# Expert gates: ScalarE's positive part plus VectorE's hundredth read from PSUM, in place of a copy and a maximum within SBUF

## What is computed

```python
def _leaky(x):
    return jnp.where(x >= 0, x, LEAKY_SLOPE * x)        # LEAKY_SLOPE = 0.01
gp = _leaky(jnp.einsum('th,ehm->etm', x, w_gate))
up = jnp.einsum('th,ehm->etm', x, w_up)
y_all = jnp.einsum('etm,emh->eth', gp * up, w_down)
p = _leaky(hidden_states @ sw_gate) * (hidden_states @ sw_up) @ sw_down
```

## Time and profile before

| | |
|---|---|
| median of 3 runs | 1069.37 us (1068.86 to 1070.07) |
| the profiled execution | 1068.73 us |
| its span in the trace | 1066.9 us |
| mean granted TensorE clock in it | 0.998 |
| busy: TensorE, VectorE, ScalarE, GpSimd | 1011.4, 725.8, 541.0, 438.6 us |
| the leak (line 1257), 80 times | 55.4 us, 692 ns each |
| the copy (line 801), 80 times | 41.2 + 6.0 us |

### The profile page before, as it was taken

One profiled execution on the slowest core, in us unless ns is written; L12 is line 12 of the kernel. 1 busy time (PEld: TensorE's weight loads), 2 busy tenths in 40 slices (PEclk: granted clock), 3 DMA queues, 4 the chain that ended last, 5 costly groups with the idle time before them and its releaser, 6 DMA issues.

```text
span 1066.9 us, 22567 instructions
## 1 busy us (share of the span) xinstructions
PE 1011.4 (95%) x7300; PEld 823.6 (77%) x7300; DVE 725.8 (68%) x2497; ACT 541.0 (51%) x1596; POOL 438.6 (41%) x422
## 2 busy tenths in 40 slices
PE   3877999999999999999999999999999999999998
PEld 2765877878787887878777787787878788787877
DVE  8889487665867558665677647766586755866543
ACT  3598256652565435663456515665256643566220
POOL 1644254441454333642535515444145433354212
PEclk9999999999999999999999999999999999999999
DMA  5326423111132013311132212311113210221043
GB/s 198 73 77 209 138 69 121 51 60 62 61 110 89 36 47 100 100 61 61 42 114 77 69 42 72 119 49 62 62 61 110 89 37 29 96 103 62 36 133 105
DMA packets 41004, 87.79 MB, mean 82 GB/s; under 512 B 4193, under 2 KB 19041, under 8 KB 40625
## 3 DMA queue, kind: packets, MB, share of 16 engines
q1 hardware_dynamic: 39920, 83.57, 23.9%
q10 hardware_dynamic: 960, 2.62, 0.7%
HBM read 76.57 MB, written 9.60 MB: 81 GB/s over the span
## 4 chain that ended last, share of the span: by engine, by line
PE 70%; DVE 15%; issue 6%; ACT 3%; DVEq 0%; POOL 0%; ACTq 0%; POOLq 0%
PE psY L1647 13%; PE psS L1517 6%; PE psO L1553 5%; PE psG L71 5%; PE psG L69 5%; PE psG L70 5%; PE psT L1528 5%; PE psS L1512 3%; PE psS L69 2%; PE psS L71 2%; PE psS L70 2%; PE psT L1535 2%; PE psO L1556 2%; DVE work L423 2%; PE psT L69 2%
## 5 line engine op out<-in xcount | busy, mean ns | idle before, releaser
L592 POOL TENSOR_TENSOR work<-work,rden 128x514 f32<-128x514 f32 x128 | 134.2, 1049 | 328.6 <-DVE rden L1143 328.1
L1647 PE MATMUL psY<-Wd,H 128*128 128x256 f32 x640 | 171.7, 397 | 0.0
L757 ACT ACTIVATE work<-work,low 128x257 f32<-128x257 f32 x256 | 128.5, 504 | 63.5 <-DVE low L1161 63.5
L69 PE MATMUL psG<-x1T_hi,Wgu 128*128 128x512 f32 (+1 forms) x292 | 134.6, 461 | 3.5 <-ACT leaky L801 1.9
L1647 PEld LDWEIGHTS psY<-Wd,H 128*128 128x128 f32 x640 | 111.6, 189 | 28.1 <-issue 14.4
L1161 DVE CUSTOM_DVE_ANT_0 work<-psS,bias,null_s 128x256 f32<-128x256 f32 x256 | 113.1, 478 | 22.3 <-PE psS L1517 19.4
L1257 DVE SCALAR_TENSOR_TENSOR leaky<-leaky 128x512 f32<-128x512 f32 x80 | 55.4, 692 | 93.3 <-ACT leaky L801 93.3
L71 PE MATMUL psG<-x1T_lo,Wgu 128*128 128x512 f32 (+1 forms) x292 | 114.7, 393 | 0.0
L70 PE MATMUL psG<-x1T_hi,Wgu 128*128 128x512 f32 (+1 forms) x292 | 113.7, 389 | 0.0
L581 POOL TENSOR_TENSOR rq<-qss,neghalf 128x16 f32<-128x16 f32 x32 | 97.5, 3049 | 34.4 <-DVE qss L1137 34.4
L761 ACT ACTIVATE work<-work,low 128x129 f32<-128x129 f32 x256 | 99.4, 390 | 0.0
(11 more groups left out here) (264 smaller groups left out, 2567.6 us busy)
## 6 DMA issues: line engine op xcount, KB each, us to landing
Wgu<-wexp SPq DMA_DIRECT2D x80, 512.0 KB, 3.4
Wb<-wscr SPq DMA_DIRECT2D x64, 256.0 KB, 3.6
wexp<-Wgu SPq DMA_DIRECT2D x10, 512.0 KB, 2.9
xres<-in_x SPq DMA_DIRECT2D x8, 512.0 KB, 4.0
xin<-in_x SPq DMA_DIRECT2D x7, 512.0 KB, 4.1
out<-work SPq DMA_DIRECT2D x7, 512.0 KB, 3.2
H<-in_wgu SPq DMA_DIRECT2D x10, 256.0 KB, 3.5
bias<-bscr SPq DMA_DIRECT2D x4, 512.0 KB, 6.2
```

The lines of the kernel that those rows point to most:

```text
L69: te.matmul(dst, a_hi, b_hi, start=start, stop=False)
L592: pool.tensor_tensor(T1[sl][:, hs, :], T1[sl][:, hs, :], rden[sl][:, 1, hs].unsqueeze(2) .to_broadcast([P, 2, N + 1]), ALU.mult)
L757: act.activation(T1[sl][:, h, :], T1[sl][:, h, :], ACT.Exp, scale=-1.0, bias=low[sl][:, 1, h:h + 1], accum_out=den[sl][:, 1, h:h + 1])
L1647: mm = te.matmul(psY[:, t // 2, (t % 2) * D:(t % 2 + 1) * D], H[:, k % H_RING, t * P:(t + 1) * P], Wd[:, ORDER[k], :], start=(k == 0 and t ...
```

## The change

ScalarE writes 0.99 times the positive part of the gate to `leaky`, and VectorE adds a hundredth of the gate, which it reads from the PSUM bank. The bank is then free for `up` only after VectorE's step, so `up` waits for `leaky_done` in place of `gate_out`; in the last stage the gate of block k waits for the leak of block k - 2.

```diff
@@ ScalarE, take_gate
-                act.activation(leaky[k % 2][:], gate_bank(k, alone), ACT.Copy) \
+                act.activation(leaky[k % 2][:], gate_bank(k, alone), ACT.Relu, scale=1.0 - LEAKY) \
                     .then_inc(gate_out.sem, 1)
@@ VectorE, leak
-            def leak(m, k):
+            def leak(m, k, alone=False):
                 need(dve, gate_out, m, k + 1)
-                dve.scalar_tensor_tensor(leaky[k % 2][:], leaky[k % 2][:], LEAKY, leaky[k % 2][:],
-                                         ALU.mult, ALU.max).then_inc(leaky_done.sem, 1)
+                dve.scalar_tensor_tensor(leaky[k % 2][:], gate_bank(k, alone), LEAKY, leaky[k % 2][:],
+                                         ALU.mult, ALU.add).then_inc(leaky_done.sem, 1)
@@ TensorE, gate
                 if alone:
-                    need(te, gate_out, m, k - 1)
+                    need(te, leaky_done, m, k - 1)
@@ TensorE, up
                 else:
-                    need(te, gate_out, m, k + 1)
+                    need(te, leaky_done, m, k + 1)
```

More of the change, by code:

```diff
@@ L1287, in _ @@
             router_shift(m)
-            leak(m, 0)
+            leak(m, 0, True)
             router_best(m)
@@ L1292, in _ @@
             for k in range(1, BLOCKS):
-                leak(m, k)
+                leak(m, k, True)
                 hidden(m, k, True)
```

## The result

The changed kernel takes **1099.84 us** (median of 4 runs, 1099.58 to 1100.76) against 1069.11 us of the kernel before on the same chip: a ratio of 1.0289, 95% interval 1.0274 to 1.0304. That is 30.7 us more, where the prediction had 29.1 (1098.5 us).

The account below looks back on a forecast made before the run. TensorE was taken to bound most of the span, VectorE a stretch of each of seven rounds. Waits of 27.4 us plus 1.7 for the clock gave 29.1 us, so 1098.5 us against the median; its own range 1094 to 1104, final range 1092 to 1107.

Parts of the forecast that it names:

- Operations at 0: ScalarE's Relu in place of Copy, and VectorE's leak reading psG, were each taken to add 0 us.
- The path: In each expert round up(0) to up(3) wait for their leak, starting 0.06 us after its end; k = 4 to 9 cost 0.
- The sum of a round: Delay of VectorE grows to 0.98, 2.24 and 3.92 us at k = 0 to 2; k = 3 covered: 3.92 us a round.
- The last round: Gates and ups have banks of their own; gate(k) waits for the leak of k-2: cost 0, otherwise about 0.7 us.
- The clock: TensorE's longer idle time before up(1) and up(2) lowers its granted clock: two falls at 0.85 us, 1.7 us.
- The sum: Whole kernel: 27.4 us of waits in seven rounds plus 1.7 us of clock, 29.1 us slower.
- A fall in every round at full price: Rival: TensorE's clock falls in all seven rounds at 1.7 us each, 39.3 us in all, 1108.7 us; chance 0.08.
- No cover at k = 3: Rival: no wait covers another, each up moves TensorE fully: 6.62 us a round, 46.3 in all, 1115.7 us; chance 0.04.
- The wait at k = 1: Rival: up(1)'s wait is hidden because something else would hold VectorE there: 2.66 us a round, 1088 us; chance 0.04.
- Not slower: Rival: VectorE has enough work between leak and hidden product for up(k) to finish in time: 1069.4 us; chance 0.03.
- A delay of VectorE in 399 to 421 moves the start of the TensorE-bound part: Stretch of a round where VectorE sets the pace; the part behind it has only 0.55 us idle in 99 to repay delays.

## Why the prediction was right

- **Operations at 0.** Right: 590 ns for Relu and 688 for the leak, and the arithmetic alone 0.9997 [0.9988, 1.0007]. The Trainium skill ("VectorE: DVE Perf Modes", section on the TRN2 errata) gives a PSUM source the larger fixed cost; the measured pair, 688 ns with psG and 690 to 692 without, has no such difference.
- **The path.** Right: up(0) to up(3) are released by their leak, 0.05 to 0.06 us after its end, where 0.06 had been taken. up(4) keeps its place: its leak has an idle wait of 1.12 us ahead of it, for ScalarE.
- **The sum of a round.** 3.92 us was forecast, 4.15 measured. From the leak's end to hidden: 1.83, 1.84 and 1.74 us for k = 0 to 2, where 0.80, 0.52 and 0.10 stood, so 1.03, 1.32 and 1.64: 3.99, against 0.98, 1.26 and 1.68. The term that was a little small is the step from up to hidden at k = 0 and 1, 1.78 us for the 1.72 read from one row before; at k = 2 it is 1.68. The rest, 0.16, is k = 3, forecast as covered: hidden(3) waits 0.48 us, as worked out, and 0.2 to 0.4 us of that came through when that wait stood alone.
- **The last round.** Right: from its hidden(0) to the end of the span are 1097.8 - 1053.72 = 44.1 us, and 1066.9 - 1022.83 = 44.1 before. The changed wait of its gates costs nothing.
- **The clock.** 2 falls at 0.85 were forecast, 1.7 us; it had 3, and with the clock held up by needless matmuls the kernel is 1.9 us better. The direction was right, number and size of the falls were a guess, and that the total came out so near is luck in part: the same waits with the arithmetic of before had seven falls, and the wait on up(2) alone six, at 1.25 each. The range had room for that. The Trainium skill ("TensorE: Matmul & The Clock Gate", section "What's actually happening") has activity release the full rate; the two runs with needless matmuls agree, with no fall in their rounds.
- **The sum.** 27.4 + 1.7 = 29.1 was forecast; the runs give 28.8 + 1.9 = 30.7. Seven rounds at 4.15 are 29.05. The term that was too small is thus the wait, by 1.4 us in all.
- **The rivals.** A fall in every round at full price would have been 1108.7 us; falls came in three of seven and cost 1.9 us together. No cover at k = 3 would have shown in the kernel with that wait alone, 1069.68. The wait at k = 1 is not hidden: alone it costs 1.3 us a round. *Not slower* would have needed 1.78 us of other work between leak and hidden; the kernel with an early leak of block 2 shows that such work does hide its up, hidden(2) there waits for nothing.
- **Where the reading was too simple.** "A delay of VectorE in 399 to 421 moves the start of the TensorE-bound part" held for the delays at k = 0 to 2. Its reverse doesn't hold: taking 1.2 us away gained 0.2. A stretch where one engine is busy 20.12 of 21.70 us can still have another engine 0.2 us behind it.

## What to carry to other kernels

An operand that is moved from SBUF to PSUM may cost nothing on the engine that reads it, and yet lengthen the time for which the bank is held. Ask who writes that bank next. The price is the time from the new last reader's end to the start of that writer, plus the time from this start to the operation that needs its result, minus what lies between the two operations of the reading engine today. Price delays and savings apart: in the tight stretch of this kernel a delay came through whole, a saving only up to the next engine. And where a new wait makes TensorE idle, add a term for its clock, whose size is less certain than the waits themselves.

## What the runs showed of the hardware

- **The clock falls by small differences.** Two kernels whose waits agree to 0.01 us in the round shown had three falls and seven; one wait of 2.78 us a round brought six, the four waits together three. Each lasted 3.4 us at 1.2 GHz and cost some 0.6 us (1.9 for three, a rough number) to 1.25 us. Matmuls that compute nothing of use removed those in the rounds, and the kernel was faster with more work: 1080.07 against 1087.58 us. What decides whether a given round falls stays open.
- **VectorE was held up by GpSimd.** With the scaling on GpSimd, its timeline has

```profile
400.70 1.91 POOL L423 TENSOR_TENSOR work<-work,rq 128x1024 f32<-128x1024 f32 x1
```

  and VectorE's score, begun at 401.99, ends at 402.66, right after GpSimd's 402.61. A round later the same: GpSimd from 527.15 to 529.06, the score from 528.44 to 529.11. Five of the eight scores are held up so, and the group of eight has a mean of 489 ns, 192 before. The Trainium skill ("SBUF — State Buffer", section "Summary: rules for kernel authors") says that where a VectorE operation has two SBUF inputs and a GpSimd operation reads SBUF, the second to issue waits until the first is done. The two rounds agree, since the score reads two SBUF tiles, and the reduction and the reciprocal just ahead of it, with one source each, kept their 0.18 us beside the same GpSimd work. But not every GpSimd operation on SBUF tiles held the score up. In the kernel before it ran beside another one, the norm rq, at its usual 0.19 us, where by that rule it would have waited until 404.12:

```profile
401.22 2.90 POOL L581 TENSOR_TENSOR rq<-qss,neghalf 128x16 f32<-128x16 f32 x1 [1.10 <-DVE qss L1137]
```

  with, on VectorE:

```profile
401.48 0.19 DVE L1211 TENSOR_TENSOR score<-lex,lrec 128x32 f32<-128x32 f32 x1
```

  What tells the two GpSimd operations apart in this, no run here shows.
